# Query weights split ahead of time, the mask on GpSimd, and output units moved in front of waits

## The reference, cut to what matters

```python
x = x + tanh(g_xattn[0]) * linear_attention(layernorm(x), ctx)      # the second stage
x = x + tanh(g_ffn[0]) * moe_lora(layernorm(x))                     # the same stage
# grouped attention of layer 1, on q = layernorm(x):
q = rope((q @ Wq).reshape(b, t, 32, 128)); k = rope((ctx @ Wk).reshape(b, t, 8, 128)); v = ctx @ Wv
logits = 30.0 * tanh(einsum('btkgd,bTkd->bkgtT', q, k) * 0.0883 / 30.0)
weights = softmax(where(mask, logits, -1e+30))                      # 4 query heads (g) to a key head (k)
x = x + tanh(g_xattn[1]) * einsum('bkgtT,bTkd->btkgd', weights, v).reshape(b, t, 4096) @ Wo
x = x + tanh(g_ffn[1]) * sign_ffn(layernorm(x))
```

## Time and profile before

| | |
|---|---|
| median of 3 runs | 3281.87 us |
| the profiled execution, its own time | 3288.88 us |
| its span, first to last instruction | 3287.1 us |
| TensorE busy | 3080.6 us, 94% of the span |
| GpSimd, VectorE, ScalarE busy | 1851.3, 2093.1, 1234.8 us |
| granted TensorE clock, mean | 0.969 |
| attention stage, first to last matmul | 1280.67 to some 3063 us |

### The profile page before, as it was taken

The page is one execution under the profiler, slowest core; times in us unless marked ns, Lnnn a source line. Parts: engine busy times, 40 slices in busy tenths (PEclk is TensorE's granted clock), DMA queues, the critical chain, the costliest instruction groups (busy, mean ns, idle before and its releaser), DMA issues. The chain is left out here.

```text
span 3287.1 us, 41110 instructions
## 1 busy us (share of the span) xinstructions
PE 3080.6 (94%) x14547; PEld 2474.0 (75%) x14547; DVE 2093.1 (64%) x2607; ACT 1234.8 (38%) x1898; POOL 1851.3 (56%) x1244
## 2 busy tenths in 40 slices
PE   7999679999999996899999999999999999998799
PEld 6888558788787775677777777777778787777577
DVE  3332357777777753767666767767777677676575
ACT  3111155555555541333333433433333434333222
POOL 4232354454454443667676767676767776764343
PEclk9999889999999997999999999999999999999799
DMA  7343501101111113222233222332222332323221
GB/s 200 107 131 109 180 26 39 65 33 65 53 45 65 52 54 114 102 90 102 89 128 141 102 95 96 121 147 96 96 96 101 129 134 96 111 90 134 84 71 52
DMA packets 171260, 315.53 MB, mean 96 GB/s; under 512 B 10328, under 2 KB 86488, under 8 KB 171144
## 3 DMA queue, kind: packets, MB, share of 16 engines
q1 hardware_dynamic: 171144, 314.04, 27.3%
HBM read 246.90 MB, written 67.11 MB: 96 GB/s over the span
## 5 line engine op out<-in xcount | busy, mean ns | idle before, releaser
L1850 DVE RECIPROCAL g_rsum<-pair 128x512 f32<-128x512 f32 x128 | 429.0, 3351 | 57.1 <-PE pair L1925 57.1
L1893 PE MATMUL pair<-g_xn_hi,g_wq_hi 128*128 128x512 f32 x1024 | 403.9, 394 | 19.1 <-POOL g_wq_lo L1569 14.0
L1893 PE MATMUL pair<-g_xn_lo,g_wq_hi 128*128 128x512 f32 x1024 | 402.5, 393 | 0.0
L1893 PE MATMUL pair<-g_xn_hi,g_wq_lo 128*128 128x512 f32 x1024 | 402.2, 393 | 0.0
L1949 PE MATMUL pair<-g_wo_hi,g_at_hi 128*128 128x512 f32 x992 | 389.6, 393 | 2.4 <-DVE g_res L1830 0.2
L1949 PE MATMUL pair<-g_wo_lo,g_at_hi 128*128 128x512 f32 x992 | 386.2, 389 | 0.0
L1949 PE MATMUL pair<-g_wo_hi,g_at_lo 128*128 128x512 f32 x992 | 386.1, 389 | 0.0
L1569 POOL TENSOR_TENSOR g_wq_lo<-g_wq_raw,g_wq_hi 128x1024 fp32r<-128x1024 f32 x130 | 310.9, 2415 | 0.0
L1569 POOL TENSOR_TENSOR g_at_lo<-g_at_raw,g_at_hi 128x512 fp32r<-128x512 f32 x128 | 180.1, 1407 | 217.6 <-ACT g_at_hi L1710 217.6
L1710 ACT ACTIVATE g_q_hi<-g_q_raw 128x512 fp32r<-128x512 f32 x128 | 81.0, 633 | 535.6 <-POOL g_q_raw L1650 535.6
L1810 DVE TENSOR_TENSOR g_q_raw<-pair,t_cos_q 128x512 f32<-128x512 f32 x128 | 88.5, 692 | 296.2 <-PE pair L1893 256.5
(11 more groups left out here) (251 smaller groups left out, 7333.3 us busy)
## 6 DMA issues: line engine op xcount, KB each, us to landing
g_wq_raw<-in_L_Wq SPq DMA_DIRECT2D x64, 1024.0 KB, 7.3
g_wo_raw<-in_L_Wo SPq DMA_DIRECT2D x62, 1024.0 KB, 6.3
values_split<-c_v SPq DMA_DIRECT2D x64, 256.0 KB, 2.8
keys_split<-c_k SPq DMA_DIRECT2D x32, 512.0 KB, 2.7
g_k<-keys_split SPq DMA_DIRECT2D x32, 512.0 KB, 3.2
g_v<-values_split SPq DMA_DIRECT2D x32, 512.0 KB, 7.7
c_cx_raw<-in_ctxT SPq DMA_DIRECT2D x16, 512.0 KB, 7.4
a_x<-in_x SPq DMA_DIRECT2D x16, 512.0 KB, 4.5
```

What stands on the lines that cost most here:

```text
L1850: V.reciprocal(rsum[:, :], p_sum[:, :]).then_inc(rsum_done, 1)
L1893: mm = M(bank[:, :], w[a][:, i, cols], x[b][:, i, :], start=(i == 0 and t == 0), stop=(i == KT - 1 and t == 2))
```

## The change

Three edits.

1. The query weights are split in the front stage. 32 pieces r of 128x1024 go through two new tiles `qp`: SP loads a piece (512 KB), ScalarE rounds it (`qp_round`), GpSimd subtracts (`qp_low`), SP stores both parts in device memory (two DMAs of 512 KB). They are placed in groups 1 to 6, six to a group (`qp_at`), so the last is r = 31 in group 6. `pass_qp` on SP first waits for piece r and stores it, and then loads piece r + 1. In the attention stage the loads take the parts (`load_wq`, four DMAs of 1 MB for a step where there were two), and the rounding of the query weights on ScalarE and their subtraction on GpSimd are gone, there and in the second stage's end. `projection` waits for the landings of the halves, and at a new group of batches `project` waits for `xn_lo`.
2. `mask_probs` goes from VectorE to GpSimd.
3. TensorE's order in `attend`: the first quarter of `out(2)` stands before `scores(n, 0)`, and half of `out(3)` before `scores(n, 2)`. In exchange only `out(5)` and half of `out(6)` stand between `values(n, 1)` and `values(n, 2)`, where there were half of `out(4)`, `out(5)` and a quarter of `out(6)`. TensorE's steps are now written by the same nested loops as the other engines' (`steps(pe, body_pe)`), with the step number made of two counters.

```diff
@@ -113,7 +118,15 @@
     k_store = [sem(f"k_store{i}") for i in range(2)]
     v_store = [sem(f"v_store{i}") for i in range(2)]
     const_pool, const_dve, const_pe = sem("const_pool"), sem("const_dve"), sem("const_pe")
-
+    qp_land, qp_store = ([sem(f"{n}{i}") for i in range(2)] for n in ("qp_land", "qp_store"))
+    qp_hi, qp_lo = sem("qp_hi"), sem("qp_lo")
+    Wq_v = Wq.rearrange("(m a p) (j n) -> j m p a n", p=P, a=2, j=NKV)
+
+
+    def qp_at(j, unit):
+
+        r = 6 * (j - 1) + unit
+        return [r] if 1 <= j <= 6 and unit < 6 and r < QP else []
     def made_v(j, i):
         return j * (PER_J + NGRP) + i + 1
@@ -181,7 +194,29 @@
                          v_sb[n % 2][:, m, :].bitcast(F32).rearrange("p (w n) -> p w n", w=VW))\
                 .then_inc(v_store[n % 2], 16)
+    def load_qp(r):
+        if r < QP:
+            after(sp, qp_store[r % 2], 32 * (r // 2))
+            sp.dma_start(qp[r % 2]["raw"].rearrange("p (a n) -> p a n", a=2), Wq_v[r // 4, r % 4])\
+                .then_inc(qp_land[r % 2], 16)
+
+    def store_qp(r):
+        sp.wait_ge(qp_lo, r + 1)
+        for i, part in enumerate(("hi", "lo")):
+            sp.dma_start(wq_out[r // 4, i, :, (r % 4) * PW:(r % 4 + 1) * PW], qp[r % 2][part][:, :].bitcast(F32))\
+                .then_inc(qp_store[r % 2], 16)
+
+    def pass_qp(j, unit):
+        for r in qp_at(j, unit):
+            store_qp(r)
+            load_qp(r + 1)
+
     A = nc.scalar.activation
+
+    def qp_round(j, unit):
+        for r in qp_at(j, unit):
+            act.wait_ge(qp_land[r % 2], 16 * (r // 2 + 1))
+            A(qp[r % 2]["hi"][:, :], qp[r % 2]["raw"][:, :], ACT.Copy).then_inc(qp_hi, 1)
     def round_hi(buf, view):
         return A(view(buf["hi"]), view(buf["raw"]), ACT.Copy)
@@ -252,6 +287,11 @@
             .then_inc(emptied, 1)
     G = nc.gpsimd
+
+    def qp_low(j, unit):
+        for r in qp_at(j, unit):
+            pool.wait_ge(qp_hi, r + 1)
+            low(G, qp[r % 2], lambda t: t[:, :]).then_inc(qp_lo, 1)
     def wv_low(q):
         for i in range(0, PIECES, 2):
@@ -324,8 +364,12 @@
             for j in range(NKV):
                 if j == NKV - 1:
                     early["pool"][0]()
+                for i in range(3):
+                    qp_low(j, i)
                 for g in range(NGRP):
                     finish_k(j, g)
+                    if g > 0:
+                        qp_low(j, g + 2)
                     if j == NKV - 1 and 1 <= g < 3:
                         early["pool"][g]()
                     if g == 0 and j == NKV // 2 - 1:
@@ -342,16 +386,24 @@
                 sp.dma_start(dst[:, :], src).then_inc(table_in, 16)
             for b in range(4, BATCH):
                 load_cx(b)
+            load_qp(0)
             for j in range(NKV):
                 for i in range(PER_J):
                     store_v(j, i)
+                    if i > 0:
+                        pass_qp(j, i - 1)
                 if j == NKV // 2 - 1:
                     load_wv(1)
                 for g in range(NGRP):
+                    if j == NKV - 1 and g == 0:
+                        for i in range(2):
+                            sp.wait_ge(qp_store[i], 32 * QP // 2)
                     if j == NKV - 1 and g < 2:
                         sp.wait_ge(made, made_k(j, g))
                         early["sync"][g]()
                     store_k(j, g)
+                    if g > 0:
+                        pass_qp(j, g + 2)
                 if j + 1 < NKV:
                     load_wk(j + 1)
             for i in range(2):
@@ -368,6 +420,8 @@
             for j in range(NKV):
                 for i in range(PER_J):
                     v_round(j, i)
+                    if i > 0:
+                        qp_round(j, i - 1)
                     if j == 0:
                         for b in range(3 * i + 4, 3 * i + 7):
                             cx_round(b)
@@ -375,6 +429,8 @@
                         wk_round(j)
                 for g in range(NGRP):
                     k_round(j, g)
+                    if g > 0:
+                        qp_round(j, g + 2)
                     if j == NKV - 1 and g < 3:
                         early["act"][g]()
                     if g == 0 and j == NKV // 2 - 1:
@@ -1573,6 +1628,14 @@
         for i in range(HALVES):
             sp.dma_start(half(name, i)(buf["raw"]), half(name, i)(src)).then_inc(land[name][i], 16)
+    def load_wq(j):
+
+        for i in range(HALVES):
+            for s, part in enumerate(("hi", "lo")):
+                src = wq_in[:, s].rearrange("j p (k n) -> j p k n", k=KT)
+                sp.dma_start(half("wq", i)(wq[part]).bitcast(F32), half("wq", i)(one(src, j)))\
+                    .then_inc(land["wq"][i], 16)
+
     def load_acts(name, buf, src, g):
         for b in range(NB):
@@ -1653,17 +1712,20 @@
     def first_pool():
-        for done in (const_pool, xn_lo, wo_lo, rot_done, rot_lo, prob_lo, at_lo, wq_lo):
+        for done in (const_pool, masked, xn_lo, wo_lo, rot_done, rot_lo, prob_lo, at_lo):
             pool.sem_inc(done, 1)
-        wq_split(0, 0)
     def first_low():
         xn_split(0, 0)
-        for m in range(1, 4):
-            wq_split(0, m)
     def body_pool(z):
         n = z.n
+
+        def mask_probs(b):
+            e = prob[b % 2]["raw"][:, :]
+            pool.wait_ge(exp_done, FIRST + n * NB + b + 1)
+            nc.gpsimd.tensor_tensor(heads(e), heads(e), keep[:, :].rearrange("p (o t) -> p o t", o=1)
+                                    .to_broadcast([P, G, SEQ]), ALU.mult).then_inc(masked, 1)
         def prob_split(b):
             pool.wait_ge(prob_hi, FIRST + n * NB + b + 1)
@@ -1673,27 +1735,21 @@
             pool.wait_ge(at_hi, FIRST + n * NB + b + 1)
             subtract_hi(nc.gpsimd, at, lambda t: t[:, :, bcols(b)]).then_inc(at_lo, 1)
-        early = not z.last and not z.group_end
+        mask_probs(0)
+        mask_probs(1)
         prob_split(0)
         prob_split(1)
+        mask_probs(2)
         attn_split(0)
         prob_split(2)
-        if early:
-            wq_split(n + 1, 0)
-            wq_split(n + 1, 1)
         if z.group_end:
             xn_split(z.g + 1, 0)
+        mask_probs(3)
         attn_split(1)
         prob_split(3)
         if z.group_end:
             xn_split(z.g + 1, 1)
-        if early:
-            wq_split(n + 1, 2)
-            wq_split(n + 1, 3)
         attn_split(2)
-        if z.group_end:
-            for m in range(4):
-                wq_split(n + 1, m)
         if z.last:
             for m in range(2):
                 wo_split(n, m, wo_last)
@@ -1761,18 +1815,10 @@
         softmax_hi(2)
         if z.group_end:
             quarters("xn", xn, z.g + 2, xn_hi, (2, 3))
-        if early:
-            quarters("wq", wq, n + 2, wq_hi, (0,))
         softmax(3)
-        if early:
-            quarters("wq", wq, n + 2, wq_hi, (1,))
         attn_hi(1)
         softmax_hi(3)
-        if early:
-            quarters("wq", wq, n + 2, wq_hi, (2, 3))
         attn_hi(2)
-        if z.group_end:
-            quarters("wq", wq, n + 2, wq_hi, range(4))
         if z.last:
             quarters("wo", wo_last, n + 1, wo_hi, range(4))
         attn_hi(3)
@@ -1887,16 +1923,18 @@
     def projection(bank, w, cols, x, fresh=None):
         for i in range(KT):
-            if fresh is not None and i % 2 == 0:
-                pe.wait_ge(wq_lo, FIRST + 4 * fresh + i // 2 + 1)
+            if fresh is not None and i % (KT // HALVES) == 0:
+                pe.wait_ge(land["wq"][i * HALVES // KT], 32 * fresh + 32)
             for t, (a, b) in enumerate(SPLIT):
                 mm = M(bank[:, :], w[a][:, i, cols], x[b][:, i, :],
                        start=(i == 0 and t == 0), stop=(i == KT - 1 and t == 2))
         return mm
-    def project(n):
-
-
+    def project(n, new_group=None):
+
+
+        if new_group is not None:
+            pe.wait_ge(xn_lo, FIRST + 2 + 4 * new_group)
         for h in range(G):
             if h == 1:
@@ -1958,22 +1996,28 @@
         out(0)
         out(1)
+        out(2, range(0, 1))
         scores(n, 0)
         scores(n, 1)
-        out(2)
+        out(2, range(1, G))
+        out(3, range(0, 2))
         scores(n, 2)
         values(n, 0)
-        out(3)
-        out(4, range(0, 2))
+        out(3, range(2, G))
+        out(4)
         scores(n, 3)
         values(n, 1)
-        out(4, range(2, G))
         out(5)
-        out(6, range(0, 1))
+        out(6, range(0, 2))
         values(n, 2)
-        out(6, range(1, G))
+        out(6, range(2, G))
         out(7)
         values(n, 3)
+
+    def body_pe(z):
+        attend(z.n, first=z.first)
+        if not z.last:
+            project(z.n + 1, z.g + 1 if z.group_end else None)
     early = {"sync": (first_wq, first_xn), "act": (first_act, first_xn_hi), "pool": (first_pool, first_low),
              "dve": (first_xn_low,)}
@@ -2042,12 +2086,7 @@
             pe.wait_ge(xn_lo_dve, 2)
             project(0)
```

(17 more changed lines are left out.)

31 lines of the change are left out of this document (12 added, 19 removed).

## The result

The changed kernel takes 3403.48 us (median of 4 runs, 3398.89 to 3409.03), the kernel before 3282.3 (3281.2 to 3283.25) on the same chip: a ratio of 1.037, interval 1.035 to 1.0391. Slower, as forecast, but by 121 us and not by 64: outside the range of 3300 to 3395.

The account below looks back on a forecast made before the run. TensorE was taken to bound the kernel. Front stage +75, second stage's end -4 and attention -7 sum to +64 on the profiled 3288.88, so 3353; the median, 7.0 lower, gives 3346 us, range 3300 to 3395.

Parts of the forecast that it names:

- What bounds the kernel: Whole kernel: TensorE, busy 94% of the span; any wait put on it in the front stage lengthens the run in full.
- The chain of pieces: Front stage: 32 pieces run one behind the other, 9.1 us a link, group period 58.3 us against 43.5; +75 us.
- from the first store's issue to the landing of the load ... I take 5.5: Front stage, part of each link: 5.5 us, between 6.0 from the nearest row and 5.1 from bandwidth.
- My long link: Front stage, slow end of the estimate: a link of 11.0 us, giving +130 us.
- The rival of the crowded queue: Front stage: landings drift to 7 us, link 10.6, stage +110 to +120, 3385 us in all; chance 0.12.
- Second stage's end: End of the second stage: GpSimd's three subtractions of query weights go, so TensorE waits less; -4 us.
- at unit 6: Attention: output unit 6 waits for VectorE's add(4), behind batch 1's reciprocal and multiply; 1.27 us a step, +39 us.
- at the first sum: Attention: with masks of 1.04 us on GpSimd the first sum's wait shrinks, -9 us; with 1.31, +6.
- the two counters: Attention: TensorE works out its wait counts from two counters in each step; +2 us, 0 to 15.
- Loads that slip past the stores: Front stage: loads move beside the stores, link 7.6 us, stage +34, 3305 us in all; chance 0.14.
- Hidden pieces: Front stage: links under 6.6 us keep up with TensorE, no waits for key weights, 3271 us in all; chance 0.06.
- A slow GpSimd in the attention: Attention: masks of 1.8 us or stalls, first sum waits 1.5 us more a step, 3390 us in all; chance 0.06.

Follow-up runs that it names:

- Experiment 4: Changed kernel with the next piece's load issued ahead of the two stores, still after the wait for the piece just split: 3362.85 us, 1.025 of the kernel before.
- experiment 2: Changed kernel with the load of piece r + 1 issued ahead of the wait for piece r and its stores: 3323.86 us, 1.012 of the kernel before.
- experiment 9: Changed kernel with next load before wait, key weights' load before a group's last piece, add(4) before normalise(1), masks on VectorE: 3240.69 us, 0.9871 of kernel before.
- experiment 6: Changed kernel with VectorE's add(4) moved ahead of normalise(1): 3357.63 us, 1.0222 of the kernel before.

## Why the prediction was wrong, point by point

**What bounds the kernel.** Right: TensorE's waits in the front stage came out of the end in full.

**The chain of pieces: right as a mechanism, and the term "from the first store's issue to the landing of the load ... I take 5.5" is the step that failed.** It is mostly 6.2 to 6.6, nearer to the rows of 1144 us, which gave 6.0, than to the bandwidth sum of 5.1 that I averaged it with. That sum gave the three transfers the peak rate. A link became 9.9 instead of 9.1; five of them and the 14.2 that holds the key weights make a period of 63.7 against the forecast 58.3, and the trace has 64.0 from wait to wait (295.10 to 359.08). Experiment 4 took the stores from the link's front and found 1.8 us. The link's missing 0.8 us, 29 times, is 23 of the 43 us by which the front stage was mis-sized; the rest is in the first group's start, in the links with weights in them, in a few longer links and in the clock:

| term of the front stage | forecast | measured |
|---|---|---|
| first group's wait | 5 | 16.8 |
| four later groups, value weights with them | 59 + 11 = 70 | 271.1 - 4 x 43.5 = 97.1 |
| slow clock behind the last wait | none | 2.6 |
| sum | 75 | 116.5 of 118.4 |

The 271.1 us are those from TensorE's first restart to its last. The first group: piece 0 was done 19 us into group 1 (15 assumed), piece 5 51.4 behind it (45), and the key weights came 12.1 us behind the last piece (9.5 assumed), since their subtraction stands behind a value unit's on the same engine. The four later groups: a period of 63.8 to 65.5 where 58.3 was forecast, and the link with the value weights is 14.2 longer than a usual one where 11 was. The third line is an omission of its own. I had counted the clock of 0.50 at the group ends and knew that waits of 15 us would come, but did not carry it into the front stage; since the chain sets the pace, it was worth 2.6 us there.

**The range.** My long link gave +130, by which the time would have been 3401, 2 us short of what came, but the range was drawn by the chances and left it out. The rival of the crowded queue had the right direction, with 7 us for the stores and the load where 6.2 to 6.6 came. Its +110 to +120 for the front stage holds the measured +118, but by luck: its longer link stands in for the late first group. Its 3385 is too low still, since the attention stage came out 13 us worse than forecast.

**The Trainium skill** ("DMA: Bandwidth & Descriptors", Specifications) puts a core's device-memory traffic at some 358 GB/s; by it each link would have been an estimated 0.7 us longer, about what it was. But the runs do not show that ceiling as the cause: from 60 to 371 us the trace's mean was 262 GB/s in experiment 2 and 274 in experiment 9, against 208 in experiment 6, whose front stage is the changed kernel's. More was moved in the same time, and the load landed in 4.4 us and not 5.5; and experiment 4 shortened the link by an order of issue alone.

**Second stage's end.** -4 forecast, -3.5 measured.

**Attention.** In the sums of TensorE's gaps over all steps: at the scores -21.8 (forecast -21); at unit 6 +42.3 (+39; the 5.45 us from sum to unit came out to the hundredth); at group ends -14.6 (-18; waits of 1.8 to 2.0 us, and behind two of the three the clock stayed at 1.00); at the first sum +2.6 (-9); and once at a last sum -2.5 (none). That is +6.0 of the +6.3, so nothing is left for the two counters (+2). The first sum is the mis-sized term: a mask takes 1.29 us, not the 1.04 of the nearest row. Line 1727 on GpSimd (count, ns min/median/max):

```profile
L1727 POOL TENSOR_TENSOR g_prob_raw<-g_prob_raw,t_keep x128: 1262/1291/1302, 1428.6 to 3119.1; 128x512 f32<-128x512 f32 x128
```

The other end that I gave, 1.31 with +6, was nearer. The Trainium skill ("GPSIMD Engine Reference", 3.1 Elementwise), whose ratio I had set aside for that row, gave an estimated 1.35 and was the better guide. The multiply of the earlier trace rows takes a spread operand too, but in another form; which part of the form makes the 0.25 us wasn't tried.

**Rivals.** Loads that slip past the stores: excluded, since stores ahead cost the load 1.0 us of landing (experiment 4). Hidden pieces: excluded for this code. A slow GpSimd in the attention, with masks of 1.8: no; yet masks there cost 19 to 27 us.

## What to carry to other kernels

Work that is moved under a stage with idle engines is hidden only if its own chain is shorter than the time it hides under: add up one link with the waits on every queue it passes, SyncE's order included, before looking at how idle the engines are. On a queue in which loads and stores share one issuer, put the load that someone waits for ahead of the stores that nobody waits for, and a small load that a later unit needs ahead of the chain, not behind it. When a unit of work is moved on one engine, look up what frees its buffer on the other engine and move that too: here a single line, `add(4)`, was worth 46 us in the changed kernel, where the moved quarters without it were worth nothing or cost 12.
